# Score products on half of the matmul array's rows, in a rewritten order of the steps

## What is computed

```
h = patches(x) @ W.T + b + pos                  # 121 tokens of 192, from 13x13 patches of 4 channels
h = concat([h, txt])                            # 121 + 128 = 249 tokens
h = h + attention(layernorm(h))
h = h + experts(layernorm(h))
# attention: 12 heads of width 16, int8 weights and activations
attn = einsum('bhnd,bhmd->bhnm', q, k) * 16 ** -0.5
attn = log_int_softmax(fq_act(attn))            # integer exponential, result rounded to a power of two
o    = einsum('bhnm,bhmd->bhnd', attn, v)
# experts: 16 experts of width 128, 4 chosen per token through 8 groups, and a shared one
y = sum_e w_e * ((silu(x @ Wu_e) * (x @ Wg_e)) @ Wd_e) + shared
```

## Time and profile before

| | us |
|---|---|
| median of 2 runs | 3519.61 |
| profiled execution, its own time | 3518.62 |
| its span | 3516.8 |
| PE busy | 3381.6 (96%) |
| DVE busy | 3368.5 (96%) |
| ACT busy | 3153.6 (90%) |
| POOL busy | 806.2 (23%) |

### The profile page before, as it was taken

The page is one execution under the profiler, slowest core; times in us unless marked ns, Lnnn a source line. Parts: engine busy times, 40 slices in busy tenths (PEclk is TensorE's granted clock), DMA queues, the critical chain, the costliest instruction groups (busy, mean ns, idle before and its releaser), DMA issues.

```text
span 3516.8 us, 98077 instructions
## 1 busy us (share of the span) xinstructions
PE 3381.6 (96%) x30764; PEld 2898.6 (82%) x30764; DVE 3368.5 (96%) x10279; ACT 3153.6 (90%) x6228; POOL 806.2 (23%) x1647
## 2 busy tenths in 40 slices
PE   1589999999999999999999999999999999999999
PEld 1368888888888888888888888888888888888888
DVE  6699999999999999999999999999999999999995
ACT  2799999999999999999999999999999999999992
POOL 3222222222222222222221221222222222222210
PEclk9789999999999999999999999999999999999999
DMA  5101001000000000000000110100000000000000
GB/s 125 27 14 25 25 16 26 25 20 23 25 20 23 24 22 21 24 23 20 25 24 18 25 25 16 26 25 17 25 25 20 23 25 21 22 24 23 20 10 8
DMA packets 157123, 85.77 MB, mean 24 GB/s; under 512 B 51451, under 2 KB 154370, under 8 KB 156610
## 3 DMA queue, kind: packets, MB, share of 16 engines
q1 hardware_dynamic: 153692, 78.82, 9.0%
q10 hardware_dynamic: 2918, 0.67, 0.1%
HBM read 54.89 MB, written 12.24 MB: 19 GB/s over the span
## 4 chain that ended last, share of the span: by engine, by line
PE 92%; DVE 1%; issue 1%; ACT 0%; POOLq 0%; DVEq 0%; POOL 0%
PE pU L1183 33%; PE pY L1209 20%; PE pX L1075 5%; PE pX L1132 5%; PE pS L1120 4%; PE pS L1111 4%; PE pS L1121 4%; PE pX L1094 3%; PE pW L1195 3%; PE pO L1142 2%; PE pY L1192 1%; PE pX L1102 1%; PE pX L1088 1%; PE pX L1151 1%; PE pX L1082 1%
## 5 line engine op out<-in xcount | busy, mean ns | idle before, releaser
L1183 PE MATMUL pU<-x2T,UG 128*128 128x250 f16 x8704 | 1231.6, 270 | 1.0 <-ACT work L676 0.9
L1183 PEld LDWEIGHTS pU<-x2T,UG 128*128 128x128 f16 x8704 | 823.0, 97 | 108.7 <-ACT work L676 1.5
L1209 PE MATMUL pY<-WD,work 128*128 128x192 f32 (+1 forms) x4352 | 810.0, 328 | 0.0
L1209 PEld LDWEIGHTS pY<-WD,work 128*128 128x128 f32 (+1 forms) x4352 | 690.8, 187 | 3.9
L962 DVE SCALAR_TENSOR_TENSOR work<-work,cst 128x249 f32<-128x249 f32 (+1 forms) x1536 | 658.6, 484 | 8.4 <-issue 4.3
L623 ACT ACTIVATE work<-work,alpha 128x249 f32<-128x249 f32 (+1 forms) x1536 | 648.3, 509 | 15.2 <-DVE alpha L974 14.0
L607 ACT ACTIVATE work<-a,room 128x249 bf16<-128x249 int8 (+1 forms) x1536 | 648.3, 514 | 0.0
L1183 PE MATMUL pU<-x2T,UGB 67*128 67x250 f16 x2176 | 592.4, 272 | 0.0
L942 DVE TENSOR_REDUCE rmax<-a 128x4 f32<-128x996 int8 (+1 forms) x384 | 452.9, 1179 | 40.9 <-ACT a L598 40.9
L632 ACT ACTIVATE passing<-pX,cst 128x512 int16<-128x512 int16 (+3 forms) x768 | 480.8, 687 | 6.9 <-PE pX L1132 3.5
L598 ACT ACTIVATE a<-pS,cst 128x996 int8<-128x996 f32 (+1 forms) x384 | 421.4, 1097 | 70.3 <-PE pS L1111 70.1
(11 more groups left out here) (209 smaller groups left out, 5337.5 us busy)
## 6 DMA issues: line engine op xcount, KB each, us to landing
img<-in_x_dram SPq DMA_DIRECT2D x896, 23.5 KB
img<-in_x_dram SPq DMA_DIRECT2D x768, 21.4 KB
qz<-qb SPq DMA_DIRECT2D x768, 15.6 KB, 1.8
h<-in_txt_dram SPq DMA_DIRECT2D x64, 96.0 KB, 2.0
out_dram<-yout SPq DMA_DIRECT2D x64, 96.0 KB
out_dram<-yout SPq DMA_DIRECT2D x64, 90.8 KB
WD<-in_L_ffn_Wd_dram SPq DMA_DIRECT2D x1, 1536.0 KB, 7.6
work<-in_L_ffn_Wu_dram SPq DMA_DIRECT2D x2, 512.0 KB, 6.6
```

The lines of the kernel that those rows point to most:

```text
L1183: a = mm(pU[:, s, q * EVEN:(q + 1) * EVEN], weights, x2T[i % 2][0:w, m, 0:EVEN], start=m == 0, stop=m == BLOCKS - 1)
L1209: a = mm(pY[0:n, t * 256:t * 256 + D], (act_[k % 2] if k else up[0])[:, c:c + n], WD[:, e, :], start=k == 0 and t == 0, stop=e == E - 1, s ...
```

## The change

Two things. The score step uses half of the array's rows for each head, rows 0 to 63 for heads 0 and 1, rows 64 to 127 for heads 2 and 3, and takes the heads in the order 0, 2, 1, 3, so that neighbours lie on different halves and in different banks. And the table `ORDER` is another one, with the same 254 entries. All lines behind the score step are one higher in the kernel after (1111 becomes 1112, 1142 becomes 1143, 1183 becomes 1184).

```diff
@@ ORDER (254 entries before and after; all of them are rewritten)
-            ("r_score", -4, -1), ("low", -3, 4), ("mmG", -5, 7), ("r_biased", -4, -1), ("weigh", -3, 3),
...
+            ("low", -2, 0), ("embed_h", -1, -1), ("gate", -4, 3), ("share", -2, 1), ("square", -2, 2),
...
@@ score
                         n, g, t = NTOK[k % 2], k // 2, k % 2
                         pe.wait_ge(qz_in[g], 16 * PER * (i + 1))
                         take_s(a_done, UNITS * i + k + 1)
-                        for m in range(PER):
+                        for m in (0, 2, 1, 3):
+                            rows = slice(m // 2 * 2 * QUAD, (m // 2 + 1) * 2 * QUAD)
                             a = mm(pS[0:n, m // 2, (m % 2) * TOKENS:(m % 2 + 1) * TOKENS],
-                                   qz[:, g * PER + m, tcols[t]], kb[:, g, :], start=True, stop=True)
+                                   qz[rows, g * PER + m, tcols[t]], kb[rows, g, :], start=True, stop=True)
                         a.then_inc(s_ps, 1)
```

More of the change, by code:

```diff
@@ L310, in fused_layer @@
[L310 to L334, removed]
@@ L340, in fused_layer @@
[L340 to L349, removed]
@@ new lines, in fused_layer @@
+            ("top", -2, 5), ("split2", -3, -1), ("stats", -1, -1), ("peak", -2, 4), ("quot", -2, 3),
+            ("mean", -1, -1), ("down", -4, 1), ("mmG", -4, 4), ("act", -4, 2), ("expo", -2, 2), ("gate", -4, 4),
+            ("turn2", -3, 0), ("grow", -2, 0), ("low", -2, 1), ("below", -2, 4), ("u", -2, 3), ("copy2", -3, 0),
+            ("mmU", -4, 5), ("square", -2, 3), ("turn2", -3, 1), ("copy2", -3, 1), ("down", -4, 2),
+            ("weigh", -2, 0), ("route", -3, -1), ("pick", -4, 3), ("sum", -2, 2), ("spread", -1, -1),
@@ new lines, in fused_layer @@
+            ("gate", -4, 6), ("r_ratio", -3, -1), ("mmU", -4, 8), ("conv", -1, 0), ("weigh", -2, 2),
+            ("qk", -1, 4), ("r_exp", -3, -1), ("alpha", -2, 4), ("square", -2, 5), ("pick", -4, 5),
+            ("power", -2, 5), ("qkq", -1, 4), ("mmG", -4, 7), ("share", -2, 3), ("turnp", -2, 1),
+            ("copyp", -2, 1), ("silu", -4, 8), ("down", -4, 4), ("act", -4, 5), ("r_sum", -3, -1),
+            ("conv", -1, 1), ("gate", -4, 7), ("r_inverse", -3, -1), ("low", -2, 3), ("pick", -4, 6),
@@ new lines, in fused_layer @@
+            ("qzload", -1, 0), ("mmG", -4, 8), ("expo", -2, 5), ("store", -5, -1), ("score", -1, 0),
+            ("qk", -1, 5), ("share", -2, 4), ("act", -4, 6), ("r_score", -3, -1), ("mmU", -3, 0),
+            ("qzload", -1, 1), ("down", -4, 5), ("sum", -2, 5), ("quant", -1, 0), ("gate", -4, 8),
+            ("score", -1, 1), ("value", -2, 1), ("qkq", -1, 5), ("silu", -3, 0), ("quant", -1, 1),
+            ("r_biased", -3, -1), ("grow", -2, 3), ("r_pairs", -3, -1), ("low", -2, 4), ("turnp", -2, 2),
@@ new lines, in fused_layer @@
+            ("pick", -4, 7), ("outq", -2, 0), ("top", -1, 0), ("down", -4, 6), ("peak", -1, 0),
+            ("r_top_pairs", -3, -1), ("weigh", -2, 3), ("act", -4, 7), ("mmU", -3, 1), ("alpha", -2, 5),
+            ("r_take_pairs", -3, -1), ("copyp", -2, 2), ("below", -1, 0), ("mmG", -3, 0), ("top", -1, 1),
+            ("pick", -4, 8), ("r_penalty", -3, -1), ("quot", -1, 0), ("act", -4, 8), ("score", -1, 2),
+            ("v", -1, -1), ("outcast", -2, 0), ("vq", -1, -1), ("value", -2, 2), ("r_masked", -3, -1),
@@ new lines, in fused_layer @@
+            ("r_part0", -3, -1), ("square", -1, 0), ("result", -4, -1), ("quot", -1, 1), ("imgload", 0, -1),
+            ("value", -2, 3), ("outq", -2, 1), ("r_rest", -3, -1), ("turnp", -2, 5), ("vconv", -1, -1),
+            ("copyp", -2, 5), ("gate", -3, 1), ("r_part1", -3, -1), ("outcast", -2, 1), ("expo", -1, 0),
+            ("r_part2", -3, -1), ("sum", -1, 0), ("down", -3, 0), ("score", -1, 3), ("mmG", -3, 2),
+            ("power", -1, 1), ("value", -2, 4), ("quant", -1, 3), ("chosen", -3, -1), ("value", -2, 5),
@@ L355, in fused_layer @@
+            ("peak", -1, 3), ("power", -1, 2), ("below", -1, 3), ("mean2", -2, -1), ("top", -1, 4),
+            ("act", -3, 1), ("share", -1, 0), ("score", -1, 5), ("spread2", -2, -1), ("quant", -1, 5),
+            ("alpha", -1, 1), ("embed", 0, -1), ("silu", -3, 4), ("pick", -3, 2), ("u", -1, 2),
+            ("norm2", -2, -1), ("txtload", 0, -1),
         ]
```

34 lines of the change are left out of this document (20 added, 14 removed).

## The result

The kernel after takes 3562.17 us (two runs, 3559.39 to 3564.95), the kernel before 3519.61. The ratio is 1.0121 [1.0077, 1.0164]. The kernel got slower by 43 us, less than the 70 us that I called a telling difference, but clear of no change by its interval, and outside the predicted range, whose upper end was 3520. The predicted 3465 us was low by 97 us.

The account below looks back on a forecast made before the run. PE bound the kernel at 52.22 us an image; with halves PE needs 50.93 and DVE, at 51.41, becomes the bound. 0.82 us over 60 images (49 us) and 6 us of fill and tail gave 3465 us, range 3442 to 3520.

Parts of the forecast that it names:

- PE is the bound, DVE right behind: Steady part before: PE's queue is the 52.22 us period, DVE needs 51.66 us an image, 0.56 us to spare.
- Pairs overlap: Score groups: two products on different halves run side by side, 0.215 us a group instead of 0.43, 1.29 us an image.
- rival 3: Score groups: halves don't overlap and the tiling change is paid, 0.65 us a group, 3602 us; chance 0.05.
- rival 4: Score groups: pairs run one after another without a price, time stays at about 3515 us; chance 0.07.
- Going over to half of the array costs the low end, nothing: Score groups: changing only the rows costs nearly nothing; the high end was up to 0.22 us a group, 1.3 an image.
- Rival 1: Score groups: halves pay the column price, 0.435 us a group, PE stays the bound, 3485 to 3520 us; chance 0.27.
- DVE's 0.25 us: Exponent instruction, line 962: the new table avoids contention with POOL's casts, saving DVE 0.25 us an image, to 51.41.
- place B: Between the first two q/k products: PE waits 0.2 to 0.4 us an image for the bank's eviction, costed at nothing.
- The SP queue, costed at nothing: The image's 26 load issues, 9.37 us, stand nearer to `embed` in the new table, but SP runs ahead: no cost.
- Rival 2: The order costs more than it saves: halves work, but DVE and PE wait 0.8 us, 3515 us; chance 0.08.

Follow-up runs that it names:

- e11: Kernel after with `chosen` moved behind value group 5, so that value groups 4 and 5 stand side by side: 3542.61 us, ratio 1.0068.
- e7: Kernel before with value groups 0 and 1, 2 and 3, 4 and 5 made neighbours in its table: 3494.06 us, ratio 0.9927.
- e1: Kernel after with the table of the kernel before, so the halves alone: 3527.39 us, ratio 1.0022.
- e5: Kernel after with the image load put behind the third `qz` load in the SP queue: 3563.33 us, ratio 1.0123.
- e2: Kernel before with the new table, score products on all 128 rows: 3563.57 us, ratio 1.0124.
- e4: Kernel after with other steps put between the q/k products of place B: 3669.27 us, ratio 1.0424.
- e8: Table of e7 with `expo` and `sum` of group 4 moved behind `act` 4: 3511.87 us, ratio 0.9977.
- e9: As e8, with `pick` 1 also moved behind `mmG` 2: 3582.2 us, ratio 1.0177.
- e3: Kernel after with the heads in the order 0, 1, 2, 3 instead of 0, 2, 1, 3: 3566.34 us, ratio 1.0129.

## Why the prediction was wrong, point by point

- **PE is the bound, DVE right behind.** Right. e11 shows the first for the new table, where 0.22 us less on PE's queue took 0.34 us off the period. e7 shows both for the table before: of 0.66 us less on PE's queue 0.41 us came out, then DVE was in the way.
- **Pairs overlap.** Right: 0.32 and 0.36 us to the successor, two rounds and the way out. That rival 3 and rival 4 fell is this.
- **Going over to half of the array costs the low end, nothing.** Wrong, and this is the first step that failed. The argument was that 67 rows cost nothing. But the product on 67 rows doesn't change the tiling: 0.11 us to its successor is the price of any full product. The row to go by was the value group, which does change it: 0.09 us in, measured on the halves as 0.09, and 0.10 out, where I had 0.13. Rival 1 priced a group at 0.435 us; measured are 0.41 and 0.45. So the 1.29 us an image that PE was to get back are nil, and e1 shows that on the old table the halves cost 0.13 us. With that the pace never went over to DVE, and the forecast fell. The Trainium skill, page "TensorEngine Tiling (Array Packing)", section "Key Properties", had the rule (a change of the tiling drains the engine, moving between tiles doesn't), and the 0.09 and 0.10 us above agree with it for tiles of 64 rows.
- **DVE's 0.25 us.** Right in sign and size: 19 of the 21 ns a piece at line 962, and 15.7 us less busy time of DVE in the whole run, 0.25 us an image, although the records of lines 983 and 948 got longer. As DVE isn't the bound, it brought nothing.
- **The wait at place B, 0.2 to 0.4 us, costed at nothing.** The wait was sized well (0.36 + 0.07 us). The step that failed is its cover: "PE has 0.48 us of room for it". I had written that without the halves' gain it costs its full price, and so it does.
- **The SP queue, costed at nothing.** `embed` isn't late, as forecast. PE does wait for `qz`, 16.8 us, which I had not looked for; it waits at another group than the one behind the image load (e5).
- **What I did not look for.** The new table's loss is 0.90 us of period in e2, (3178.7 - 310.1) / 54 = 53.12 us against 52.22. The start distances of all of PE's groups, averaged over these periods, add up to the two periods, so they show where the 0.90 us stand:

  | where in PE's queue | us an image, e2 against before |
  |---|---|
  | place B, behind the eviction at line 643 | +0.36 and +0.07 |
  | the first score group, for `qz` (nothing in half of the images, up to 2 us in others) | +0.36 |
  | f32 groups behind short products: `embed` behind a score group | +0.10 |
  | down groups behind a value group (0.10) and behind transposes (0.05 each, four places instead of two) | +0.21 |
  | a down group ahead of line 1082, whose weight load starts late for a reason that the profile doesn't name | +0.10 |
  | `chosen` between two value groups, `u` behind one, products ahead of a `turnp` | +0.14 |
  | waits of weight loads in the earlier trace rows that are gone | -0.36 |
  | all other places together | -0.08 |

  So PE's waits for ACT and for the load of `qz` are 0.79 us of it, and the prediction had costed the first at nothing and had no row for the second. The table is read from two traces and not tested place by place: e4 removed place B and brought more elsewhere, and e5 moved a load at which PE doesn't wait. That the new order does it, e2 shows; what each place would give if it were mended stays open.
- **The rivals.** Rival 1 had the halves right, and allowed for the table at worst 0.4 us on PE; with the wait for `qz` and the neighbours of the f32 loads it is over twice that. Rival 2, "the order costs more than it saves", named the right culprit, and its 0.8 us of waits are near what PE waits here. But it put them between DVE and PE and on top of halves that work; the waits are for ACT's eviction and for `qz`, and DVE has room. None of my rivals lay between 3520 and 3590 us, as I never added rival 1 and rival 2. That sum, 52.2 + 0.8 us, would have given some 3560 us. That it meets the measured 3562 is in part luck, as the 0.8 us was no count of these waits.

The best version measured is e7, 3494.06 us: 0.7% faster than the kernel before, and 1.9% faster than the kernel after (3494.06 against 3562.17).

## What to carry to other kernels

When one engine goes through its queue without a stop, judge a new order on that engine's queue first: take each pair of neighbours that is new, and price it by the start distance of such a pair in the trace (a tiling that is entered and left, a long weight load behind a short product). Then look for what the queue will wait for: a bank that must be emptied, a chain of cast and load that must be through. The second part is the harder one. Three runs that moved a few steps to remove one wait or collision (e4, e8, e9) each made new waits elsewhere and lost 107, 18 and 70 us. Work on a part of the array pays when many such products stand together, since the way in and out, 0.2 us here, is paid per group and not per product; four products of 249 columns only break even, and putting value groups side by side gained 25 us, where the halves gained nothing. Two rivals that don't exclude each other are a third one: add them before you set the range.

## What the runs showed of the hardware that was not expected

- The order of products on the two halves makes no difference (e3): heads 0, 1, 2, 3 take the same 0.32 and 0.36 us as 0, 2, 1, 3. If a half does one product at a time, the array takes the other half's product ahead of its turn; the records don't say which head a product belongs to, so this is inferred. The Trainium skill, page "TensorE: Matmul & The Clock Gate", section "The mechanism" of Part 3, says that matmuls start and end in program order. Two pairs in e3 don't fit that, and the measurement decides.
- A group with 121 columns of output takes 0.36 us, one with 128 takes 0.32: the smaller weights cost 0.04 us more. Their weight loads take 131 ns in the mean, those of 128 columns 95 ns. On the full array a group takes 0.43 us with either, though the loads differ there too (137 and 105 ns).
- The f32 weight load shows behind short products or another tiling: down 1.41 instead of 1.31 us behind a value group, 1.40 behind a half; `embed` 3.43 us behind a full score group and 3.53 behind a half, instead of 3.33 behind a product of 498 columns.
- An instruction that is moved away from one collision of DVE and POOL can meet the next: in e8 the exponent group left the first group's casts and met the second's (a record of 0.65 us at 1807.87), and line 962 stayed at 498 ns.
